# Three PSUM banks for the quads of a graph-attention loop, and one VectorE pass for a quad's keys

## The chip, the cores and the metric

One core of one Trainium2 chip runs the whole program. The metric is the device time of one execution in microseconds (us), the median over several executions.

## The reference

Four graph layers over 3,125 nodes of 64 features and 100,000 edges sorted by destination, each followed by a residual addition and a layer norm. The change lies in the last one, an attention whose logit of an edge is linear in the source row, the destination row and two edge attributes:

```python
z = h @ W_fc.T
a = z_src @ blk[0] + z_dst @ blk[K] + ex @ w_e      # + moment terms, the same for all edges
att = jnp.where(a > 0, a, SLOPE * a)
m = jax.ops.segment_max(att, dst, num_segments=N)
expv = jnp.exp(att - m[dst])
denom = jax.ops.segment_sum(expv, dst, num_segments=N)
w = expv / denom[dst]
msg = w[:, None] * (z_src + ez)
return jax.ops.segment_sum(msg, dst, num_segments=N)
```

## The kernel before

The last attention handles the edges in tiles of 128, 16 tiles (UT) to a unit, 49 units. Two kinds of unit run side by side.

**The first 28 units (ND)** need no gathered rows. A tile's weights are spread by one-hot matrices: `low_w` (128 edges by 128 low bits of the source, weighted) and `keys_w` (128 edges by 25*6 = 150 columns: high bits of the source and place of the destination in a window of 6). Their product over a quad of four tiles (QT) is summed in one PSUM bank of 25*20 = 500 columns; `weigh` on TensorE first clears the bank with a matmul by zeros (L2798), then makes the four products (L2806, each fp32 product is two instructions of the trace). VectorE adds the finished quad into `blocks` (`add_quad`, L2518). When the unit's four quads are added, `block_sum` (L2840) multiplies `blocks` with the node table `tab` and VectorE adds the result into `acc` (L2577).

**The other 21 units (NPU)** are gathered. GpSimd issues 16 indirect DMAs a unit (L2284), 334 in all, of rows of `att_tab[1]` into a ring of 7 slots (SLOTS), in a loop of its own; it waits for the landing of the first two of each four, and, from the eighth unit on, for the sum of the unit seven before. VectorE takes the logits out of the landed rows (`logits_p`: L2458, L2460, L2462) after waits on that unit's landings, ScalarE takes their exponents (L2679), VectorE scales one-hot windows (`hots_p`, L2503), TensorE sums (`gathered_sum`, L2829) and VectorE adds (L2570). Which gathered unit j is dealt with in which pass i of the main loop is the list `beside_of`: three in each four passes; unit 4 in pass 4, unit 11 in pass 13, unit 17 in pass 21, unit 20, the last, in pass 25.

The orders of the main loop are written by hand. VectorE in pass i: `turn_lo(i+2)` (L2349), `logits_d(i+1)` (L2467, L2470, L2472 and the three lines of the logits), `add_sums(i-1)`, `keys(i,2)`, `add_quad` 0, `keys(i,3)`, `add_quad` 1, 2 and 3, `keys(i+1,0)`, `keys(i+1,1)`, then `logits_p` and `hots_p` of the gathered unit. A call of `keys` first makes what `attributes` makes (L2485, L2487, after a wait for the products of the quad two before, since the rings of `low_w` and `keys_w` hold eight tiles) and then the four key tiles (L2511), each with a semaphore of its own. TensorE in pass i: `weigh(i)`, `sources(i+2)` (L2772), `block_sum(i)`, `gathered_sum`. Before quad m may clear its bank, TensorE waits until quad m-2 has been added: the banks 2 and 3 take turns. ScalarE makes `low_w` of three tiles of a quad (L2651, L2658), clears `blocks` and takes the exponents.

Bank 1 is used before the loop and in it only by a check of limits in passes 3 and 4. The banks 4 and 6 take the block sums (columns 0 to 87) by turns, 5 and 7 the gathered ones.

Of the kernel before, what the change touches and what calls it, by code (L numbers as in the profile page):

```python
# [8 lines left out]
ALU, ACT, AX = mybir.AluOpType, mybir.ActivationFunctionType, mybir.AxisListType  # L9

P = 128
N, D, E = 3125, 64, 100000
H, DH = 4, 16
NT = -(-N // P)
# [20 lines left out]
UT = 16  # L35
TW = 6
QT, QW = 4, 20
UW = 88
KH = NT * TW
# [4 lines left out]
LOW_RING = 8  # L44
# [22 lines left out]
def build(nc, x, src, dst, edge_attr_2, edge_attr_64, Wq, bq, Wk, bk, We, be, Wv, bv,  # L67
          attn_w, W_fc, W_attn, W_edge, W_e2n, W_m1, W_m2, out):
    ctx = ExitStack()
    with ctx:  # L70
        def sb(name, shape, dt=fp32):
            return ctx.enter_context(nc.sbuf_tensor(name, shape, dt))
# [7 lines left out]
        def short_sem(name):  # L80


            return nc.alloc_semaphore(name=name)

        def bc(ap, axis, n):

            ap = ap.unsqueeze(axis)
            shape = list(ap.shape)
            shape[axis] = n
            return ap.to_broadcast(shape)  # L90
# [20 lines left out]
        ident = sb("ident", [P, P])  # L111
# [65 lines left out]
        bank = [ctx.enter_context(nc.psum_tensor(f"bank{i}", [P, 512], fp32)) for i in range(8)]  # L177
# [771 lines left out]
        worst, worst_t = short_sem("worst_ready"), short_sem("worst_turned")  # L949
# [871 lines left out]
        def from_big(*shape):  # L1821

            size = int(np.prod(shape))
            view = big[:, at_big[0]:at_big[0] + size]
            at_big[0] += size
            assert at_big[0] <= big.shape[1]
            names = "abcd"[:len(shape)]
            return view if len(shape) == 1 else view.rearrange(f"p ({' '.join(names)}) -> p {' '.join(names)}", **dict(zip(names, shape)))

        TD = ND * UT  # L1830
        lo_t, hi_t, key_t = (from_big(TD) for _ in range(3))
# [26 lines left out]
        keys_w = shared[:, at_sh:at_sh + LOW_RING * KH].rearrange("p (r n) -> p r n", r=LOW_RING)  # L1858
# [13 lines left out]
        iota_k = shared[:, at_sh:at_sh + KH]  # L1872
# [12 lines left out]
        drift, drift2, root_of, extra_m, lim, lims, worst = (stage[:, a:b] for a, b in ((56, 57), (57, 58), (58, 59), (59, 60), (256, 264), (264, 280), (280, 288)))  # L1885
# [300 lines left out]
        def l2_pool(pool):  # L2186
# [19 lines left out]
        lo_ok3, u_ok3, u_used, arg_d, prob_d, arg_p, prob_p, attr_ok, hot_p, key_ok3, low_ok, main_ok, quad_added, cleared3, sum_d, rows_moved, sum_p, sum_p_added, ea_put = (  # L2206
            short_sem(f"e_{n}") for n in ("lo", "u", "u_used", "arg_d", "prob_d", "arg_p", "prob_p", "attributes", "hot_p", "key", "low", "main",
                                          "quad_added", "cleared", "sum_d", "rows_moved", "sum_p", "sum_p_added", "ea_put"))
# [25 lines left out]
            return slice((ND + i) * UT, (ND + i) * UT + tiles_of(i))  # L2234

        mean_cols = bank[7][:, D:D + 2]
        XP = [range(j, min(j + 4, -(-NT // 2))) for j in range(0, -(-NT // 2), 4)]

        ZG = [range(0, 14, 2), range(1, 14, 2), range(15, NT, 2), range(14, NT, 2)]
# [4 lines left out]
        def copy_x(engine, k):  # L2244


            js = XP[k]
            full = [j for j in js if 2 * j + 1 < NT]
# [24 lines left out]
        with nc.Block() as block:  # L2273
# [42 lines left out]
            def _(dve):  # L2316
# [40 lines left out]
                for g, ks in enumerate(WG):  # L2357
                    dve.wait_ge(win_ok, g + 1)
                    n, of = len(ks), slice(0, min(P, TL - ks[0] * P))
# [116 lines left out]
                def attributes(i, q):  # L2476

                    n, s = i * UT + q * QT, i % 2
                    at = n % LOW_RING
                    if q == 0:  # L2480
                        dve.wait_ge(prob_d, i + 1)
                    if n >= LOW_RING:
                        dve.wait_ge(main_ok, n + QT - LOW_RING)
                    last = at + QT - 1
                    nc.vector.tensor_scalar(low_w[:, last, 0:FREE], iota[:, 0:FREE], lo_t[:, n + QT - 1:n + QT], cols_d[:, 1, s, (q + 1) * QT - 1:(q + 1) * QT],  # L2485
                                            ALU.is_equal, ALU.mult).then_inc(attr_ok, 1)
                    nc.vector.tensor_tensor(low_w[:, at:at + QT, FREE:P], ea_t[:, n:n + QT, :], bc(cols_d[:, 1, s, q * QT:(q + 1) * QT], 2, 2),  # L2487
                                            ALU.mult).then_inc(attr_ok, 1)
# [16 lines left out]
                def keys(i, q):  # L2505

                    attributes(i, q)
                    for n in range(i * UT + q * QT, i * UT + (q + 1) * QT):
                        if n >= LOW_RING:
                            dve.wait_ge(main_ok, n - LOW_RING + 1)  # L2510
                        nc.vector.tensor_scalar(keys_w[:, n % LOW_RING, :], iota_k, key_t[:, n:n + 1], None, ALU.is_equal).then_inc(key_ok3, 1)  # L2511

                def add_quad(i, q, at):

                    n = i * (UT // QT) + q
                    dve.wait_ge(main_ok, (n + 1) * QT)
                    into = blocks[:, i % 2, :, bass.ds(at, QW)]
                    nc.vector.tensor_tensor(into, into, bank[2 + n % 2][:, 0:NT * QW].rearrange("p (h w) -> p h w", w=QW), ALU.add).then_inc(quad_added, 1)  # L2518
                    dve.drain()

                def registers(ap, most):
# [25 lines left out]
                def choose(i):  # L2547


                    if i == CHECK_AT:  # L2550
                        nc.vector.tensor_reduce(lims[0:5, 8:9], bank[1][0:5, 96:96 + P], AX.X, ALU.max)
                        nc.vector.tensor_scalar(lims[0:5, 9:10], ident[0:5, 4:5], -1.0, 1.0, ALU.mult, ALU.add)
                        nc.vector.tensor_copy(lims[0:5, 10:11], ident[0:5, 4:5])
                        dve.drain().then_inc(lim_top, 1)
                    if i == CHECK_AT + 1:
                        nc.vector.tensor_copy(worst[0:1, 0:2], bank[1][0:1, 96:98])
                        dve.drain()
                        nc.vector.tensor_scalar(worst[0:1, 2:3], worst[0:1, 0:1], SPREAD, None, ALU.is_gt)
                        dve.drain()
                        nc.vector.tensor_tensor(worst[0:1, 3:4], worst[0:1, 2:3], worst[0:1, 1:2], ALU.max)  # L2560
                        dve.drain()
                        nc.vector.tensor_copy(flag_i[:, 2:3], worst[0:1, 3:4])
# [140 lines left out]
            def _(pe):  # L2703
                for k, js in enumerate(XP):
                    for i, j in enumerate(js):
                        n = min(2, NT - 2 * j) * D
                        last = nc.tensor.transpose(bank[k][0:n, i * P:(i + 1) * P], xrow[:, 2 * j:2 * j + n // D, :].rearrange("p t f -> p (t f)"), ident[:, :])
                    last.then_inc(x_up, 1)
                for t in range(NT):
# [3 lines left out]
                    i = ZG[k].index(t)  # L2713
# [44 lines left out]
                def registers(ap, most):  # L2758

                    return nc.values_load_multi_w_load_instructions(ap, engines=[mybir.EngineType.PE], min_val=0, max_val=most,  # L2760
                                                                    skip_runtime_bounds_check_because="tables_dve holds them in this range")[1]
# [28 lines left out]
                def weigh(i):  # L2790

                    for q in range(UT // QT):
                        m = i * (UT // QT) + q
                        at = registers(quad_at[:, m * QT:(m + 1) * QT], QW - TW)
                        if m >= 2:
                            pe.wait_ge(quad_added, m - 1)
                        into = bank[2 + m % 2]
                        nc.tensor.matmul(into[:, 0:NT * QW], zeros_b[:, :], zero_cols(NT * QW), start=True, stop=False, skip_group_check=True)  # L2798
                        for j in range(QT):
                            n = m * QT + j  # L2800
                            if j == 0:
                                pe.wait_ge(attr_ok, 2 * (m + 1))
                            pe.wait_ge(key_ok3, n + 1)
                            if j < QT - 1:
                                pe.wait_ge(low_ok, m * (QT - 1) + j + 1)
                            nc.tensor.matmul(into[:, 0:NT * QW].rearrange("p (h w) -> p h w", w=QW)[:, :, bass.ds(at[j], TW)], low_w[:, n % LOW_RING, :],  # L2806
                                             keys_w[:, n % LOW_RING, :].rearrange("p (h w) -> p h w", w=TW), start=False, stop=j == QT - 1,
                                             skip_group_check=True).then_inc(main_ok, 1)

                def check_limits(i):  # L2810

                    if i == CHECK_AT:
                        pe.wait_ge(lim_ok, 1)
                        nc.tensor.transpose(bank[1][0:5, 96:96 + P], lim[:, 0:5], ident[:, :])
                    if i == CHECK_AT + 1:
                        pe.wait_ge(lim_top, 1)
                        nc.tensor.matmul(bank[1][0:1, 96:98], lims[0:5, 8:9], lims[0:5, 9:11], start=True, stop=True)

                def gathered_sum(j):

# [180 lines left out]
```

## Time and profile before

| | |
|---|---|
| median of 3 executions | 1918.82 us (1913.54 to 1918.93) |
| the profiled execution | 1916.29 us, span of its instructions 1914.5 us |
| VectorE busy | 1417.2 us, 74% |
| TensorE busy | 1365.9 us, 71% |
| GpSimd busy | 1241.5 us, 65% |
| main loop of the last attention | from 1458 to 1880 us of the span |

The busy shares are means over four layers with different limits. The loop of the last attention takes some 420 us of the span; what the change does is read there. Times in the rows are in us from the start of the span, of one profiled execution.

### The profile page before, as it was taken

To read this page: it belongs to the slowest core of one execution; us is meant where nothing else is said; L and a number is where in the kernel's file an instruction comes from. 1 tells how busy PE (TensorE), PEld (TensorE's weight loads), DVE (VectorE), ACT (ScalarE), POOL (GpSimd) and SP (SyncE) were. 2 spreads that over 40 slices of the span, in tenths; PEclk is the share of its full clock that TensorE was granted. 3 is DMA by queue.
4 is the path that set the end of the run, shared out by engine and by line. 5 is a ranking of instruction groups with operands and counts; after the bars stand their busy time and mean duration, and the time that the engine had idled before them with its cause. 6 is when DMAs were issued, how large, how long until landed. Compare 5 with 4: busy or idle time off the path is not lost. (4 is left out here: it accounts for less than half of the span.)

```text
span 1914.5 us, 44162 instructions
## 1 busy us (share of the span) xinstructions
PE 1365.9 (71%) x12903; PEld 1155.2 (60%) x12903; DVE 1417.2 (74%) x3785; ACT 1007.7 (53%) x2221; POOL 1241.5 (65%) x1328
## 2 busy tenths in 40 slices
PE   4476676676676767677776478648676788898884
PEld 3355555555555555555555378638576778888784
DVE  5777777777777777777777788788855777777774
ACT  2454444454454454454454295039724677777771
POOL 1677777777777777777777186025537777777740
PEclk8678878878888888888888688869966999999996
DMA  6333333333333333333332221000232222223210
GB/s 102 99 77 82 83 76 83 82 76 83 81 77 82 82 77 82 82 77 82 83 77 74 65 58 60 4 1 2 86 82 51 61 61 60 62 61 71 62 21 18
DMA packets 125228, 128.65 MB, mean 67 GB/s; under 512 B 80959, under 2 KB 88435, under 8 KB 124840
## 3 DMA queue, kind: packets, MB, share of 16 engines
q0 software_dynamic: 35776, 62.74, 15.9%
q1 hardware_dynamic: 63778, 57.41, 9.9%
q10 hardware_dynamic: 25542, 6.81, 1.6%
q8 instruction: 75, 1.23, 0.3%
q14 instruction: 57, 0.47, 0.1%
HBM read 116.64 MB, written 10.20 MB: 66 GB/s over the span
## 5 line engine op out<-in xcount | busy, mean ns | idle before, releaser
L636 POOL DMA_INDIRECT shared<-kv_tab,idx x784 | 767.7, 979 | 289.7 <-issue 237.7
L839 PE MATMUL bank<-key_hot,lo_hot 128*128 128x350 f16 x784 | 185.0, 341 | 299.2 <-DVE count L700 245.9
L2284 POOL DMA_INDIRECT count<-att_tab,count x240 | 237.4, 989 | 111.4 <-issue 70.7
L839 PEld LDWEIGHTS bank<-key_hot,lo_hot 128*128 128x128 f16 x784 | 56.0, 98 | 386.4 <-issue 371.2
L700 DVE TENSOR_TENSOR count<-count,bank 128x350 f32 x392 | 205.2, 523 | 82.4 <-issue 43.2
L772 ACT ACTIVATE lo_dist<-iota_neg,tile_lo 128x128 f16<-128x128 f32 x784 | 238.5, 389 | 0.0
L685 DVE TENSOR_SCALAR key_hot<-iota_key,tile_key 128x350 f16<-128x350 f16 x784 | 196.1, 320 | 0.0
L706 DVE TENSOR_TENSOR prod<-bank,shared 128x512 f32<-128x512 f32 x98 | 67.7, 691 | 149.1 <-DMA shared<-kv_tab,idx 141.0
L2806 PE MATMUL bank<-shared 128*128 128x150 f32 x896 | 159.4, 327 | 1.8 <-DVE shared L2511 1.8
L2658 ACT ACTIVATE shared<-shared 128x126 f32<-128x126 bf16 x336 | 143.3, 483 | 31.2 <-PE bank L2806 25.1
L814 PE MATMUL bank<-webd,eaT 128*128 128x128 f32 x784 | 159.1, 368 | 0.6 <-ACT eaT L766 0.6
L782 ACT ACTIVATE expo<-score 128x32 f32<-128x32 f32 x98 | 22.5, 229 | 254.7 <-DVE score L718 254.7
L854 PE MATMUL bank<-hots,msg 128*65 128x64 f32 x1568 | 154.7, 274 | 0.0
L854 PEld LDWEIGHTS bank<-hots,msg 128*65 128x65 f32 x1568 | 152.2, 189 | 0.4 <-DVE msg L727 0.4
L2806 PEld LDWEIGHTS bank<-shared 128*128 128x128 f32 x896 | 142.8, 216 | 15.0 <-issue 4.0
L766 ACT ACTIVATE eaT<-bank 128x512 f32<-128x512 f32 x98 | 58.6, 598 | 177.0 <-issue 177.0
L814 PEld LDWEIGHTS bank<-webd,eaT 128*128 128x128 f32 x784 | 145.6, 278 | 1.0 <-ACT eaT L766 1.0
L778 ACT ACTIVATE lo_hot<-lo_dist,small 128x1024 f16<-128x1024 f16 x98 | 112.5, 1148 | 25.5 <-issue 25.5
L822 PE MATMUL bank<-qwin,hotT 128*128 128x128 f32 x784 | 114.4, 289 | 0.0
L2840 PE MATMUL bank<-count,tab 128*68 128x88 f32 x1400 | 111.7, 240 | 1.8 <-DVE count L2518 1.8
L822 PEld LDWEIGHTS bank<-qwin,hotT 128*128 128x128 f32 x784 | 95.7, 192 | 25.3 <-issue 25.3
L2284 POOL DMA_INDIRECT g_edge<-att_tab,count x94 | 90.9, 967 | 29.3 <-issue 27.1
(528 smaller groups left out, 2974.7 us busy)
## 6 DMA issues: line engine op xcount, KB each, us to landing
shared<-in_edge_attr SPq DMA_DIRECT2D x97, 256.0 KB, 3.1
shared<-lo_tab SPq DMA_DIRECT2D x28, 512.0 KB
shared<-kv_tab,idx POOLq DMA_INDIRECT x784
count<-att_tab,count POOLq DMA_INDIRECT x240, 2.5
qwin<-q_tab ACTq DMA_DIRECT2D x196, 16.0 KB
kv_tab<-count SPq DMA_DIRECT2D x1, 1600.0 KB, 10.4
idx<-in_src SPq DMA_DIRECT2D x97, 4.0 KB, 1.6
g_edge<-att_tab,count POOLq DMA_INDIRECT x94
```

What stands on the lines that cost most here:

```text
L636: nc.gpsimd.indirect_dma_start(kv[:, s, c, :], None, kv_tab, bass.IndirectOffsetOnAxis(ap=idx[:, s, c:c + 1], axis=0)).then_inc(kv_in[s], 16)
L685: last = nc.vector.tensor_scalar(key_hot[:, c, :], iota_key[:, :], keys[:, c:c + 1], None, ALU.is_equal)
L700: nc.vector.tensor_tensor(at, at, bank[6 + q % 2][:, 0:KC].rearrange("p (h w) -> p h w", w=WC), ALU.add).then_inc(bank_free, 1)
L772: nc.scalar.activation(lo_dist[:, c, :], iota_neg[:, :], ACT.Abs, bias=los[:, c:c + 1])
L778: nc.scalar.activation(lo_hot[:, :, :], lo_dist[:, :, :], ACT.Relu, bias=edge_col, scale=-EDGE).then_inc(lo_ok, 1)
L814: nc.tensor.matmul(bank[3][:, q * P:(q + 1) * P], eaT[:, q * P:(q + 1) * P], webd[:, :], start=q == 0, stop=False, skip_group_check=True)
L822: last = nc.tensor.matmul(bank[4][:, c * D:(c + 2) * D], hotT[:, c // 2, :], qwin[:, s, :, :].rearrange("p a f -> p (a f)"), start=True, s ...
L839: last = nc.tensor.matmul(bank[6 + q % 2][:, 0:KC], lo_hot[:, c, :], key_hot[:, c, :], start=i == 0, stop=i == GT - 1)
L854: last = nc.tensor.matmul(bank[5][0:D + 1, 0:W], msg[:, c, :], hots[:, s % 2, c, :], start=c == 0, stop=c == C - 1)
L2284: nc.gpsimd.indirect_dma_start(ring[s][:, j, 0:D + 2], None, att_tab[1], bass.IndirectOffsetOnAxis(ap=src_i[:, t:t + 1], axis=0)).then_inc ...
L2658: nc.scalar.activation(low_w[:, n % LOW_RING, 0:FREE], low_dist[:, n % LOW_RING, 0:FREE], ACT.Relu, bias=p, scale=minus_p).then_inc(low_ok, 1)
L2806: nc.tensor.matmul(into[:, 0:NT * QW].rearrange("p (h w) -> p h w", w=QW)[:, :, bass.ds(at[j], TW)], low_w[:, n % LOW_RING, :], keys_w[:, ...
```

## The change

Three things are edited.

1. `quad_banks = (2, 3, 1)`: the quads take three banks by turns. TensorE waits for the addition of quad m-3 before it clears, where it waited for that of quad m-2.
2. The four `tensor_scalar` instructions of a quad's keys (128x150 each, one input, its compare value a column) become one `tensor_tensor` of 128x600 with two broadcast inputs, and one semaphore step. TensorE waits once for a quad's keys, ahead of the first product. The wait on `main_ok` inside the loop goes; the one in `attributes`, for the same ring, stays.
3. The check of limits moves from bank 1 to columns 96 and up of bank 4 or 6.

```diff
+        quad_banks = (2, 3, 1)
...
                     attributes(i, q)
-                    for n in range(i * UT + q * QT, i * UT + (q + 1) * QT):
-                        if n >= LOW_RING:
-                            dve.wait_ge(main_ok, n - LOW_RING + 1)
-                        nc.vector.tensor_scalar(keys_w[:, n % LOW_RING, :], iota_k, key_t[:, n:n + 1], None, ALU.is_equal).then_inc(key_ok3, 1)
+                    n = i * UT + q * QT
+                    at = n % LOW_RING
+                    nc.vector.tensor_tensor(keys_w[:, at:at + QT, :], bc(iota_k, 1, QT), bc(key_t[:, n:n + QT], 2, KH), ALU.is_equal).then_inc(key_ok3, 1)
...
-                    nc.vector.tensor_tensor(into, into, bank[2 + n % 2][:, 0:NT * QW].rearrange("p (h w) -> p h w", w=QW), ALU.add).then_inc(quad_added, 1)
+                    nc.vector.tensor_tensor(into, into, bank[quad_banks[n % 3]][:, 0:NT * QW].rearrange("p (h w) -> p h w", w=QW), ALU.add).then_inc(quad_added, 1)
...
-                        nc.vector.tensor_reduce(lims[0:5, 8:9], bank[1][0:5, 96:96 + P], AX.X, ALU.max)
+                        nc.vector.tensor_reduce(lims[0:5, 8:9], bank[4 + 2 * (i % 2)][0:5, 96:96 + P], AX.X, ALU.max)
...
-                        nc.vector.tensor_copy(worst[0:1, 0:2], bank[1][0:1, 96:98])
+                        nc.vector.tensor_copy(worst[0:1, 0:2], bank[4 + 2 * (i % 2)][0:1, 96:98])
...
-                        if m >= 2:
-                            pe.wait_ge(quad_added, m - 1)
-                        into = bank[2 + m % 2]
+                        if m >= 3:
+                            pe.wait_ge(quad_added, m - 2)
+                        into = bank[quad_banks[m % 3]]
...
                             if j == 0:
+                                pe.wait_ge(key_ok3, m + 1)
                                 pe.wait_ge(attr_ok, 2 * (m + 1))
-                            pe.wait_ge(key_ok3, n + 1)
...
-                        nc.tensor.transpose(bank[1][0:5, 96:96 + P], lim[:, 0:5], ident[:, :])
+                        nc.tensor.transpose(bank[4 + 2 * (i % 2)][0:5, 96:96 + P], lim[:, 0:5], ident[:, :])
...
-                        nc.tensor.matmul(bank[1][0:1, 96:98], lims[0:5, 8:9], lims[0:5, 9:11], start=True, stop=True)
+                        nc.tensor.matmul(bank[4 + 2 * (i % 2)][0:1, 96:98], lims[0:5, 8:9], lims[0:5, 9:11], start=True, stop=True)
```

## Rows read from the trace of the kernel before

**Rows 1.** The page's part 1: busy us (share of the span) xinstructions, by engine.
```profile
PE 1365.9 (71%) x12903; PEld 1155.2 (60%) x12903; DVE 1417.2 (74%) x3785; ACT 1007.7 (53%) x2221; POOL 1241.5 (65%) x1328
```

**Rows 2.** Windows in the loop: stretch, its length, busy us by engine, clock, DMA.
```profile
1600.00:1700.00 100.00, 89.67 (x1092) 82.97 (x1088) 78.45 (x275) 75.39 (x192) 74.48 (x78) 0.93 0.29 65
1700.00:1800.00 100.00, 90.25 (x1117) 83.22 (x1116) 77.35 (x268) 74.35 (x191) 75.00 (x77) 0.94 0.28 64
```

**Rows 3.** Waits of the loop, 1460 to 1880: waiter <- releaser: total, times, longest.
```profile
PE bank L2798 <- DVE count L2518: 44.1, 47, 7.0
DVE count L2518 <- PE bank L2806: 28.4, 30, 2.0
POOL count L2284 <- DMA count<-att_tab,count: 6.1, 7, 2.0
```

**Rows 4.** Timeline of VectorE in a pass: start, duration, instruction, [idle before <- releaser].
```profile
1660.36 0.35 DVE L2485 TENSOR_SCALAR shared<-iota,count,shared 128x126 f32<-128x126 f32 x1 [0.16 <-issue]
...
1671.20 0.92 DVE L2511 TENSOR_SCALAR shared<-shared,count 128x150 f32<-128x150 f32 x4
1672.04 0.67 DVE L2518 TENSOR_TENSOR count<-count,bank 128x500 f32 x1
1672.90 0.67 DVE L2518 TENSOR_TENSOR count<-count,bank 128x500 f32 x1 [0.20 <-issue]
1674.38 0.68 DVE L2518 TENSOR_TENSOR count<-count,bank 128x500 f32 x1 [0.81 <-PE bank L2806]
```

**Rows 5.** Timeline of TensorE in that pass.
```profile
1670.83 0.38 PE L2798 MATMUL bank<-zeros_b 128*128 128x500 f16 x1 [1.49 <-ACT shared L2658]
...
1672.98 1.26 PE L2806 MATMUL bank<-shared 128*128 128x150 f32 x8
1674.07 1.36 PE L2772 MATMUL bank<-shared,ad_row 128*128 128x25 bf16 x48
1675.28 3.99 PE L2840 MATMUL bank<-count,tab 128*68 128x88 f32 x50
```

**Rows 6.** VectorE timeline: two tensor_tensor instructions, fp32, inputs in SBUF.
```profile
1454.16 0.97 DVE L2451 TENSOR_TENSOR count<-count,edge_scratch 128x784 f32<-128x784 f32 x1
...
1664.83 0.57 DVE L2467 TENSOR_TENSOR shared<-count,iota 128x400 f32<-128x400 f32 x1
```

**Rows 7.** GpSimd timeline: last gathers of units 4, 11, 17 and 20, and two longer ones.
```profile
1521.68 0.94 POOL L2284 DMA_INDIRECT count<-att_tab,count  x1 [0.30 <-issue]
...
1617.80 1.00 POOL L2284 DMA_INDIRECT count<-att_tab,count  x1 [0.30 <-issue]
...
1663.79 1.24 POOL L2284 DMA_INDIRECT count<-att_tab,count  x1 [0.30 <-issue]
...
1666.58 0.94 POOL L2284 DMA_INDIRECT count<-att_tab,count  x1 [0.30 <-issue]
...
1791.17 0.94 POOL L2284 DMA_INDIRECT count<-att_tab,count  x1 [0.30 <-issue]
...
1849.37 0.94 POOL L2284 DMA_INDIRECT g_edge<-att_tab,count  x1 [0.30 <-issue]
```

**Rows 8.** VectorE timeline: first logits instruction of gathered units 4, 11, 17 and 20.
```profile
1542.58 0.17 DVE L2458 TENSOR_TENSOR shared<-count 128x16 f32<-128x16 f32 x1
...
1677.66 0.16 DVE L2458 TENSOR_TENSOR shared<-count 128x16 f32<-128x16 f32 x1
...
1794.98 0.18 DVE L2458 TENSOR_TENSOR shared<-count 128x16 f32<-128x16 f32 x1 [1.27 <-DMA count<-att_tab,count]
...
1852.79 0.18 DVE L2458 TENSOR_TENSOR shared<-g_edge,count 128x14 f32<-128x14 f32 x1
```

**Rows 9.** VectorE timeline: the last pass, two of its waits.
```profile
1869.75 0.34 DVE L2485 TENSOR_SCALAR shared<-iota,count,shared 128x126 f32<-128x126 f32 x1 [0.89 <-PE bank L2806]
...
1875.20 0.68 DVE L2518 TENSOR_TENSOR count<-count,bank 128x500 f32 x1 [0.80 <-PE bank L2806]
```

**Rows 10.** TensorE timeline: a quad's products after a long wait, in pass 3.
```profile
1518.47 2.21 PE L2806 MATMUL bank<-shared 128*128 128x150 f32 x8
```

## The prediction

> **What bounds the kernel now.** I read the page first, then windows, waits and timelines of the last attention, since only that loop (1458 to 1880) is touched. The page's shares [rows 1] name no bound. In two stretches of the loop TensorE is busy 90% and VectorE 78%, at a granted clock of 0.93 and 0.94 of full speed, nearly always the higher level [rows 2]; GpSimd is busy 75%, and that turns out to matter most.
>
> The waits point at the two banks: TensorE's clearing matmul waited 44.1 us for `add_quad`, and `add_quad` waited 28.4 us for the products [rows 3]. One pass shows how these join. VectorE begins a chain at 1660.36, and it runs nearly without a gap until the second addition, 1672.04 to 1672.71. Only then may TensorE clear the bank of the fourth quad, whose products run 1672.98 to 1674.24. The third addition is long done, and VectorE has been idle for 0.81 us when it starts the fourth at 1674.38, which ends at 1675.06 [rows 4, 5]. Behind it stand `block_sum` (1675.28) and the next pass. Between passes VectorE's order closes the ring: it is VectorE's work plus one trip to TensorE, some 14.86 us, where a pass has a gathered unit beside it. (The 1.49 us before the third quad's clearing is ascribed to ScalarE [rows 5], but the first addition, which the two-bank rule names, ended just before 1670.83.)
>
> There is a second ring, which neither edit touches. GpSimd issues the gathers one after the other, 0.94 to 0.95 us each and 0.30 us of issue between them. Its waits for landings make 6.1 us in 7 [rows 3], and the waits list none for a ring slot, so nothing that VectorE or TensorE do earlier makes it earlier. How far ahead is it? The last gather of unit 4 ends at 1522.62 and its logits begin at 1542.58: 20.0 us ahead. Unit 11: 1667.52 and 1677.66, 10.1 us. Unit 17: 1792.11 and 1794.98, and here VectorE waited 1.27 us for the landing. Unit 20, the last: 1850.31 and 1852.79, 2.5 us [rows 7, 8]. A landing takes up to some 2.9 us after the gather (unit 17, which did wait), so the lead is 17 us at unit 4 and nothing at 17 and 20. The loop already catches up with the gathers at its end.
>
> **The change part by part.**
>
> *Three banks.* The fourth quad need no longer wait for the second addition: its bank was freed by the addition of the first. Its products can start when its keys are there and the third quad's products are done. In the pass above the keys end at 1672.12 [rows 4], the products take 1.26 us [rows 5] and would end by 1673.5; VectorE meanwhile does the second and third additions and, after 0.20 us of its own issue, is ready for the fourth at 1673.77. The 0.81 us of idle time shrinks to these 0.20: 0.61 us a pass. What is late next is VectorE itself.
>
> *One pass for the keys.* The four old instructions take from 1671.20 to the start of the addition at 1672.04, 0.84 us, and show 0.92 us from first start to last end, since neighbours overlap by 0.08 [rows 4]. The trace has no 128x600 instruction of this form, but it has the same form at 400 columns, compare and two broadcast inputs included: 0.57 us; and a plain one at 784: 0.97 us [rows 6]. The line between them has 1.04 ns a column and gives 0.78 us at 600. Against 0.92 that is 0.14 us a quad. The bounds: all of the 784-column row (0.97, a loss of 0.05 a quad) and 0.57 + 0.10 (half the slope for the added columns, a gain of 0.25). I take 0.14, since the near row is the same operation. The wait for the gathers covers most of this term: only four quads come after it, so 0.97 us would move the end by 4 x 0.19 = 0.8 us; with that cover gone it would be 112 quads, 21 us. TensorE now waits for all four keys before the first product, where it could take them one by one; in the old order that freedom was unused, since the clearing came after all keys and an addition. Behind that wait stand the quad's four products; here it costs at most the order I have counted already.
>
> Together: 0.61 + 4 x 0.14 = 1.17 us a pass, and 28 x 1.17 = 33 us if the loop could have it all. TensorE has room for it: in that pass it was idle for 1.49 us before the third quad [rows 5].
>
> *The moved check* is one transpose, one small matmul and their readers in another bank, in the same places of the orders: nothing.
>
> *Where the gain meets the gathers.* Pass i runs up to 1.17 x (i+1) us earlier. By pass 9 or 10 this is 11 to 13 us, while the lead falls from 17 us (unit 4, pass 4) to 7 (unit 11, pass 13). From there on `logits_p` waits for its rows, a wait on VectorE with `hots_p` and the whole next pass queued behind it, and TensorE's `gathered_sum` behind that. Each later gain is given back at the next gathered unit. The logits of unit 20 cannot begin before the last gather's landing, and that stood at 1852.79 at most, at 1850.31 at least [rows 7, 8]. I take 0.2 us of this 2.5, since unit 17's landing took 2.9.
>
> *What is left* is what comes after unit 20: quads 2 and 3 of pass 26 and the fourth addition's idle time, 2 x 0.14 + 0.61, and the same in pass 27, where the same 0.80 us of idle time stands before the fourth addition [rows 9]. The keys of its quads 0 and 1 give nothing, because VectorE waits 0.89 us for TensorE after them [rows 9]. So 0.89 + 0.89 = 1.78, with the 0.2 above 1.98 us.
>
> *GpSimd's own pace* can shift the whole by a little. Some 24 gathers were stretched by 0.04 to 0.09 us while the old key instructions ran (one: 1.00 instead of 0.94) [rows 7]. If the new form doesn't, at most 1.2 us comes back; I take 0.6. The waits for landings (6.1 us, of which 0.30 each is issue) may fall otherwise by 2 or 3 us either way, since every transfer of the stage shifts. One at 1663.79, stretched to 1.24 us, is of another kind: it lies over `turn_lo`, a copy-like pass over 2,048 bf16 columns, and that stays.
>
> The sum: 1.98 + 0.6 = 2.6 us, so 1916.29 - 2.6 = 1913.7 for the profiled execution. The median of the runs is 2.5 us above that execution, which would give 1916.2; with single runs from 1913.54 to 1918.93 I take 1915.
>
> **The rivals.**
>
> *The full gain arrives.* If the gathers kept ahead all the same, 28 x 1.17 = 33 us: 1883. Against it stands that GpSimd works at 1.25 us a gather through the loop, and would have to issue its 334 gathers in some 30 us less.
>
> *GpSimd speeds up by itself.* Its landings fall better and the stretches go: 6 to 10 us, 1908 to 1912. It would need most of its landing waits to vanish.
>
> *Slower: the new form holds GpSimd back.* A gather reads its indices in SBUF, and the new keys instruction reads two SBUF inputs. If it blocks a gather as `turn_lo` does (0.30 us over the usual 0.94 [rows 7]), some 96 quads lie within the remaining gathers, and if each hits one, they end 29 us later: 1942. It decides from 0.03 us a quad on, where it eats my 2.6 us. Against it: the row of the same form at 400 columns (1664.83 to 1665.40 [rows 6]) lies over the gathers of its time, of which only the one before it, over `turn_lo`, was long.
> The Trainium skill, "SBUF — State Buffer", section "Who interferes with whom", states both sides: a VectorE instruction with two SBUF inputs contends with a GpSimd instruction that reads SBUF, whereas `tensor_scalar` can take a mode that locks the shared ports outright and `tensor_tensor` has none. By the first, this rival would hold; by the second, GpSimd would lose some stretches. The trace agrees with the second for bf16 `turn_lo` and shows next to nothing for the fp32 keys.
>
> *TensorE's clock.* TensorE will now stand idle ahead of the last gathered sums, for `hots_p`. After a wait of some 7 us the products of a quad took 2.21 us instead of 1.26 [rows 5, 10], the lower of the two levels (1.2 against 2.4 GHz). If that hits the fourth quads of passes 26 and 27, about 1 us each goes: no change at all, 1916 to 1918.
>
> **Chances.** The forecast (bound by the gathers, within 5.7 us of before, the clock's case with it): 0.75. GpSimd faster by itself: 0.11. The full gain or a large part: 0.06. GpSimd held back or another loss over 0.3%: 0.08. A measurement of this kernel tells about 0.3%, 5.7 us. So faster 0.17, same 0.75, slower 0.08. The range takes in GpSimd's faster case and 2 to 3 us of bad landings: 1908 to 1921; what it leaves out is the 0.06, most of the 0.08 and some edge.
>
> **What would show it.** VectorE's wait in front of the logits (L2458) on the gathers, 1.27 us before, should total some 20 to 30 us from the unit of pass 9 or 10 on. The idle time before `add_quad` should fall below half, the waits of the clearing matmul for `add_quad` should nearly vanish. The keys instruction should take 0.78 us. The last gather should end within 3 us of 1850.3. The prediction is wrong if the gathers end much earlier or later, or if `logits_p` doesn't wait.

## The result, and the profile after

The changed kernel takes 1931.81 us (median of 8, 1925.22 to 1935.70), the kernel before 1918.88 us (median of 8, 1913.54 to 1924.84). The ratio is 1.0061, with a 95% interval of 1.0041 to 1.0082: some 12 us slower. The forecast was 1915 us and no change, with a range of 1908 to 1921 us.

The profiled execution of the changed kernel took 1934.55 us, its span is 1932.8 us, 18.3 us more than before. Three stretches add up to that:

| stretch of the span | before | after | difference |
|---|---|---|---|
| start to the first gather | 1416.1 | 1420.8 | +4.7 |
| first gather's start to the last one's end | 434.3 | 448.4 | +14.2 |
| last gather's end to the end | 64.2 | 63.6 | -0.6 |

The first line is code that wasn't edited. Over the other profiled executions with all their gathers that start lies between 1414.5 and 1424.4, with no order in it; it is this execution's share of the spread between runs. The second line is the change.

VectorE's and TensorE's own part went as intended. The timeline of VectorE in a pass after the change, then TensorE's of the same pass:

```profile
1705.59 0.78 DVE L2511 TENSOR_TENSOR shared<-shared,count 128x600 f32<-128x600 f32 x1
1706.29 0.67 DVE L2518 TENSOR_TENSOR count<-count,bank 128x500 f32 x1
1707.15 0.68 DVE L2518 TENSOR_TENSOR count<-count,bank 128x500 f32 x1 [0.20 <-PE bank L2806]
1708.03 0.68 DVE L2518 TENSOR_TENSOR count<-count,bank 128x500 f32 x1 [0.20 <-PE bank L2806]
```

```profile
1703.73 0.37 PE L2798 MATMUL bank<-zeros_b 128*128 128x500 f16 x1
1704.71 1.28 PE L2806 MATMUL bank<-shared 128*128 128x150 f32 x8 [0.60 <-DVE shared L2511]
1705.83 0.37 PE L2798 MATMUL bank<-zeros_b 128*128 128x500 f16 x1
1706.50 1.29 PE L2806 MATMUL bank<-shared 128*128 128x150 f32 x8 [0.30 <-DVE shared L2511]
```

The keys take 0.78 us. The third and fourth clearing matmuls no longer wait (over the whole loop their waits for additions, 44.1 us before [rows 3], are gone), and TensorE now waits for the keys. The idle time before the fourth addition is 0.20 us where it was 0.81 [rows 4, 5].

What VectorE waits for in the loop, after (answering to [rows 3]):

```profile
DVE shared L2459 <- DMA count<-att_tab,count: 32.1, 7, 6.5
DVE shared L2486 <- PE bank L2806: 13.7, 16, 1.3
DVE acc L2577 <- issue: 12.9, 26, 0.9
DVE count L2518 <- PE bank L2806: 11.5, 50, 1.1
DVE shared L2459 <- DMA g_edge<-att_tab,count: 11.5, 4, 4.6
```

L2459 is the first instruction of `logits_p`. It waited 43.6 us for gathered rows, in 11 waits, where it had waited 1.3 us in one. So the time won was handed to the gathers, as forecast, and from gathered unit 5 (pass 5) on, earlier than the pass 9 or 10 that I gave; in the kernel with the banks only, below, the first long wait is in pass 9. VectorE's and TensorE's busy shares in the two stretches of [rows 2] fell accordingly:

```profile
1600.00:1700.00 100.00, 82.69 (x952) 77.44 (x953) 64.96 (x166) 68.91 (x174) 76.92 (x76) 0.86 0.26 59
1700.00:1800.00 100.00, 85.48 (x1012) 78.68 (x1011) 70.90 (x184) 73.35 (x189) 75.67 (x76) 0.91 0.27 64
```

The logits of units 11, 17 and 20 (answering to [rows 8]) stand behind waits of 4.6 to 6.5 us, and the last gather starts at 1868.27 where it started at 1849.37 [rows 7], 18.9 us later, where the forecast allowed 3:

```profile
1683.82 0.18 DVE L2459 TENSOR_TENSOR shared<-count 128x16 f32<-128x16 f32 x1 [6.49 <-DMA count<-att_tab,count]
...
1810.46 0.18 DVE L2459 TENSOR_TENSOR shared<-count 128x16 f32<-128x16 f32 x1 [5.41 <-DMA count<-att_tab,count]
...
1871.36 0.18 DVE L2459 TENSOR_TENSOR shared<-g_edge,count 128x14 f32<-128x14 f32 x1 [4.56 <-DMA g_edge<-att_tab,count]
```

```profile
1868.27 0.94 POOL L2285 DMA_INDIRECT g_edge<-att_tab,count  x1 [0.30 <-issue]
```

Why are the gathers slower? Their groups, of the changed kernel and of the kernel before, in the stretch 1400 to 1900 (count, busy us, mean ns, idle before):

```profile
L2285 POOL DMA_INDIRECT count<-att_tab,count x240 | 246.4, 1027 | 110.0 <-issue 69.8 <-DMA att_tab<-tab 34.0 <-DMA count<-att_tab,count 5.7
L2285 POOL DMA_INDIRECT g_edge<-att_tab,count x94 | 95.3, 1014 | 30.7 <-issue 27.7 <-DMA g_edge<-att_tab,count 2.7 <-DMA count<-att_tab,count 0.3
```

```profile
L2284 POOL DMA_INDIRECT count<-att_tab,count x240 | 237.4, 989 | 111.4 <-issue 70.7 <-DMA att_tab<-tab 34.7 <-DMA count<-att_tab,count 6.1
L2284 POOL DMA_INDIRECT g_edge<-att_tab,count x94 | 90.9, 967 | 29.3 <-issue 27.1 <-DMA g_edge<-att_tab,count 2.2
```

The idle times are the same; the instructions are longer, by 246.4 + 95.3 - 237.4 - 90.9 = 13.4 us. Set beside VectorE's timeline, it is plain which ones. GpSimd, then VectorE, after:

```profile
1716.75 0.94 POOL L2285 DMA_INDIRECT g_edge<-att_tab,count  x1 [0.30 <-issue]
1718.00 1.03 POOL L2285 DMA_INDIRECT g_edge<-att_tab,count  x1 [0.30 <-issue]
1719.33 1.49 POOL L2285 DMA_INDIRECT g_edge<-att_tab,count  x1 [0.30 <-issue]
1721.13 0.94 POOL L2285 DMA_INDIRECT g_edge<-att_tab,count  x1 [0.31 <-issue]
```

```profile
1717.44 0.78 DVE L2511 TENSOR_TENSOR shared<-shared,count 128x600 f32<-128x600 f32 x1
...
1719.23 0.78 DVE L2511 TENSOR_TENSOR shared<-shared,count 128x600 f32<-128x600 f32 x1
```

The gather of 1719.33 starts 0.10 us into a keys instruction that has 0.68 us to go, and takes 1.49 us, 0.55 more than its neighbours. The one of 1718.00 meets the last 0.22 us and takes 0.09 more. Counted over the whole trace, 50 of the 334 gathers start under a keys instruction; 36 of them have more than 0.13 us of it to go, and all but one of these are longer than 0.945 us by that rest less 0.11 to 0.13 us. Together it is 13.5 us. A gather under which a keys instruction starts later is not longer, but for one of 68, which is recorded as starting 0.03 us ahead of the instruction and is 0.71 us longer. So a gather that starts under the instruction waits for its end.

The old keys held gathers by the same rule, only for less. The gather of 1617.80 in the kernel before, one of the two longer ones of [rows 7], took 1.00 us. It started 0.10 us into this instruction, with 0.18 us to go:

```profile
1617.70 0.28 DVE L2511 TENSOR_SCALAR shared<-shared,count 128x150 f32<-128x150 f32 x1
```

Of the 53 gathers there that started with more than 0.13 us of an old keys instruction to go, 27 are longer by that rest less 0.12 to 0.14 us, together 1.4 us. Another 23 started within 0.06 us of the instruction's own start and are longer by 0.02 us at most. The last 3 are 0.21 to 0.31 us longer, and two of these also meet `turn_lo`.

A gather is held only to the end of the instruction under which it starts, although the next one of the four starts 0.08 us before that end. So four instructions of 0.29 us hold one by 0.13 us at most, and one of 0.78 us holds it by up to 0.63.

`turn_lo`, 0.75 us long and with one SBUF input, holds a gather that starts under it by the same rule (9 of 14 in the kernel before; the other 5 started within 0.04 us of its start). It also holds gathers already under way: the one of 1663.79 [rows 7] started 0.37 us before it and ends 0.12 us after it. Of the 15 gathers that `turn_lo` met so, 11 were longer, and each of these ended 0.12 us after it.

### The profile page after: what moved, and what is told of

The parts are those of the page before. It is cut to its first block and busy times, and to the rows that moved or that the text cites. A ratio compares the mean times of both kernels' runs of the same rounds, so it can differ in the third digit from the quotient of the medians.

```text
span 1932.8 us, 43602 instructions
## 1 busy us (share of the span) xinstructions
PE 1382.7 (72%) x12903; PEld 1183.8 (61%) x12903; DVE 1400.0 (72%) x3449; ACT 1008.6 (52%) x2221; POOL 1253.3 (65%) x1328
## 5 line engine op out<-in xcount | busy, mean ns | idle before, releaser
L839 PE MATMUL bank<-key_hot,lo_hot 128*128 128x350 f16 x784 | 180.3, 334 | 292.0 <-DVE count L700 244.9
L2285 POOL DMA_INDIRECT count<-att_tab,count x240 | 246.4, 1027 | 110.0 <-issue 69.8
L2806 PEld LDWEIGHTS bank<-shared 128*128 128x128 f32 x896 | 146.7, 218 | 45.2 <-issue 38.3
L854 PE MATMUL bank<-hots,msg 128*65 128x64 f32 x1568 | 167.0, 288 | 0.0
L854 PEld LDWEIGHTS bank<-hots,msg 128*65 128x65 f32 x1568 | 165.4, 203 | 0.4 <-DVE msg L727 0.4
L2285 POOL DMA_INDIRECT g_edge<-att_tab,count x94 | 95.3, 1014 | 30.7 <-issue 27.7
```

Source lines behind the costliest of these rows:

```text
L839: last = nc.tensor.matmul(bank[6 + q % 2][:, 0:KC], lo_hot[:, c, :], key_hot[:, c, :], start=i == 0, stop=i == GT - 1)
L854: last = nc.tensor.matmul(bank[5][0:D + 1, 0:W], msg[:, c, :], hots[:, s % 2, c, :], start=c == 0, stop=c == C - 1)
L2285: nc.gpsimd.indirect_dma_start(ring[s][:, j, 0:D + 2], None, att_tab[1], bass.IndirectOffsetOnAxis(ap=src_i[:, t:t + 1], axis=0)).then_inc ...
```

## The experiments

Theory G: the gathers bind the loop, and the new keys instruction stretches the gathers that start under it, because it reads two inputs from SBUF. Rival B: the three banks or the new order of waits slow the loop itself. Rival P: the loss lies ahead of the loop.

| kernel | median us | ratio to before (95%) | gathers: us, stretch | logits waited |
|---|---|---|---|---|
| before | 1918.88 | 1 | 434.3, 12.9 | 1.3 |
| changed | 1931.81 | 1.0061 (1.0041 to 1.0082) | 448.4, 26.6 | 43.6 |
| banks only | 1916.30 | 0.9986 (0.9965 to 1.0007) | 434.1, 12.5 | 21.3 |
| keys only | 1930.59 | 1.0070 (1.0049 to 1.0092) | 452.8, 31.4 | 32.1 |
| keys only, one input in PSUM | 1914.26 | 0.9982 (0.9963 to 1.0001) | 431.0, 12.6 | 13.5 |
| changed, half the gathers | 1869.46 | 0.9756 (0.9728 to 0.9783) | 380.9, 24.6 (168 of them) | 0 |
| before, half the gathers | 1914.58 | 0.9977 (0.9956 to 0.9998) | 367.1, 8.4 (168) | 0 |

Each ratio is to runs of the kernel before on the same chip (medians 1918.7 to 1920.3 us); it is not the quotient of two medians, and lies up to some 0.002 from it. Stretch is the sum over all gathers of the time above 0.945 us. Some 12 us of it stand in each kernel with all its gathers, most of it from other lines: in the kernel before 5.6 us belong to gathers held by `turn_lo`.

**Banks only.** The changed kernel with the old keys, and TensorE waiting for them one by one as before:

```diff
-                    nc.vector.tensor_tensor(keys_w[:, at:at + QT, :], bc(iota_k, 1, QT), bc(key_t[:, n:n + QT], 2, KH), ALU.is_equal).then_inc(key_ok3, 1)
+                    for n in range(i * UT + q * QT, i * UT + (q + 1) * QT):
+                        if n >= LOW_RING:
+                            dve.wait_ge(main_ok, n - LOW_RING + 1)
+                        nc.vector.tensor_scalar(keys_w[:, n % LOW_RING, :], iota_k, key_t[:, n:n + 1], None, ALU.is_equal).then_inc(key_ok3, 1)
...
-                                pe.wait_ge(key_ok3, m + 1)
...
+                            pe.wait_ge(key_ok3, n + 1)
```

> Three banks and the moved check, the keys in four tensor_scalar instructions as before. Theory G (the loop is bound by GpSimd's gathers, and the new keys instruction stretches those gathers that start under it): the gathers take 434 us from the first start to the last end, as before, and the time is that of before or 1 to 3 us less (1916 to 1919). Rival B (the three banks or the new order of waits make the loop slower): the time stays near that of the changed kernel, 10 us or more above before. Rival P (the loss comes from ahead of the loop, where nothing was edited): first gather late by 4 us or more here too.

As theory G has it. The banks cost nothing; what they win, VectorE spends waiting for rows, in the logits:

```profile
DVE shared L2459 <- DMA count<-att_tab,count: 19.2, 5, 5.0
```

**Keys only.** The kernel before, with the one-pass keys and its single wait on TensorE; banks 2 and 3.

> Two banks as before, the keys in one tensor_tensor. Theory G: some 0.3 to 0.4 of a gather in each ten is stretched, the gathers take 10 to 15 us longer than in before (445 to 449), time 8 to 14 us above before. Rival B: the time of before, or a few us less by 4 x 0.14 us a pass.

The whole loss is back with the keys alone. 55 gathers start under the instruction and are 18.4 us longer in sum; the gathers take 452.8 us, somewhat more than the 445 to 449 expected. Banks only has shown that the three banks do no harm. This kernel has the single wait for four keys as well, so it leaves open whether that wait does; the next one settles it. Rival P falls here: the first gather starts at 1416.9, within 1 us of before, and the loss is there.

**Keys only, one input in PSUM.** As above, with the check of limits moved as in the change, and:

```diff
+        iota_ps = bank[1][:, 0:KH]
...
+                nc.vector.tensor_copy(iota_ps, iota_k)
+                dve.drain()
...
-                    nc.vector.tensor_tensor(keys_w[:, at:at + QT, :], bc(iota_k, 1, QT), bc(key_t[:, n:n + QT], 2, KH), ALU.is_equal).then_inc(key_ok3, 1)
+                    nc.vector.tensor_tensor(keys_w[:, at:at + QT, :], bc(iota_ps, 1, QT), bc(key_t[:, n:n + QT], 2, KH), ALU.is_equal).then_inc(key_ok3, 1)
```

> Two banks (2 and 3); the keys in one tensor_tensor as in the changed kernel, but its first input, the 150 column numbers, is read from PSUM bank 1, so that it has one SBUF input like the addition of a quad, under which no gather was stretched. Theory G: the stretches under the keys vanish (0 us), the gathers take 432 to 436 us, time that of before or up to 2 us less. If instead the length of the instruction or its one pass does the harm, whatever its inputs: 8 to 14 us above before, as with the keys alone.

The instruction is as long as before, and harmless. Its group, and a gather that starts 0.10 us into one, with 0.68 us to go, like that of 1719.33 above:

```profile
L2513 DVE TENSOR_TENSOR shared<-bank,count x112: 768/776/784, 1460.0 to 1869.1; 128x600 f32<-128x600 f32 x112
```

```profile
1632.26 0.78 DVE L2513 TENSOR_TENSOR shared<-bank,count 128x600 f32<-128x600 f32 x1
```

```profile
1632.36 0.94 POOL L2285 DMA_INDIRECT count<-att_tab,count  x1 [0.30 <-issue]
```

64 gathers start with more than 0.13 us of such an instruction to go and are 1.0 us longer in sum, against 13.5 us for 36 in the changed kernel. All of the 1.0 us is in four gathers under which `turn_lo` starts next, and each ends 0.12 us after `turn_lo`. Length, number and order are those of the keys-only kernel. Only the place of one input differs, beside the check in passes 3 and 4 and one copy ahead of the loop. The single wait on TensorE is there too and does no harm, so rival B has fallen, and with it my remark in the forecast that this wait might matter. The gathers take 431.0 us, 1 less than expected. The time is 3.5 us below before by the ratio, where I had up to 2, and its interval still takes in no change.

The Trainium skill ("SBUF — State Buffer", section "Who interferes with whom") states this rule: a VectorE instruction with two SBUF inputs contends with a GpSimd instruction that reads SBUF. The traces agree with it, 13.5 us against 1.0.

So theory G holds but for its reason. That both inputs lie in SBUF is needed for the new form to hold gathers. It isn't what sets the new form apart from the old, which reads one input from SBUF and holds them too; that is its length. The new compare in four pieces of 150 columns would show how much is length alone, and was not run.

**Half the gathers.** The changed kernel, with the tiles 2 and 3 of each four of a gathered unit left out:

```diff
+                for s in range(SLOTS):
+                    nc.gpsimd.memset(ring[s][:, :, 0:D + 2], 1.0)
+                pool.drain()
...
+                        if j % 4 > 1:
+                            continue
...
-                        if j % 4 == 3:
+                        if j % 4 == 1:
...
-                    dve.wait_ge(rows3_last[j % SLOTS], last_rows(j, n))
```

> The changed kernel with half the gathers left out (tiles 2 and 3 of each four of the 21 gathered units; their places in the ring are filled with ones once), so its output differs. Theory G: GpSimd is far ahead, the logits never wait, and the loop shows its own speed: a pass of 13.7 us with a gathered unit and 11.4 without, 30 us or more below before (1880 to 1890), although the keys instruction is the same. If the loop itself had become slower or the gathers were not its bound: the time stays within 10 us of the changed kernel, above before.

No wait for rows is left, and the stretched gathers (24.6 us over 168) cost nothing. The time is 10 us and more below the expected 1880 to 1890.

**Half the gathers, before.** The same edit in the kernel before.

> The kernel before (two banks, four key instructions) with the same half of the gathers left out and the ring filled with ones once, so its output differs. Theory G: the loop's own ring, 14.9 us a pass with a gathered unit, is what binds, and the gathers cost it only the 1.3 us of one wait: 1905 to 1917, and 31 to 38 us above the changed kernel with half the gathers (28 passes by 0.61 + 4 x 0.14 us, and fewer stretches at the lower clock). If half the gathers alone explained the gain of that run, the two would lie within 10 us.

The time is in the expected range, the distance to the kernel above is not: 1914.58 to 1869.46 is 45 us. What the change does to the loop when no gather binds it is less than that. From the start of the first block sum to that of the last it is 403.5 us before and 368.2 after, 35.3 us over 27 passes; the forecast had 27 x 1.17 = 31.6. The two profiled executions are 46.1 us apart. Of the rest 6.7 us lie ahead of the first block sum, 5.2 of them ahead of the first gather where nothing was edited, and 4.0 behind the last, with no cause shown. Passes with a gathered unit take 13.6 to 14.3 us from pass 7 on, but for the last of them; one of 13.67 us, seen from the starts of two block sums in the changed kernel with half the gathers:

```profile
1796.79 3.99 PE L2844 MATMUL bank<-count,tab 128*68 128x88 f32 x50
1810.46 3.99 PE L2844 MATMUL bank<-count,tab 128*68 128x88 f32 x50
```

The forecast's steps give 14.86 - 1.17 = 13.69.

**Moving the bound.** If the gathers bind, work should go from GpSimd to the loop. ND says how many units are dense; each step takes 16 gathers away and adds a pass. The edit is one constant, in three forms of the kernel:

| ND | before | banks only | changed |
|---|---|---|---|
| 28 | 1 | 0.9986 | 1.0061 |
| 29 | | 0.9901 (0.9875 to 0.9926), 1901.67 us | 0.9953 (0.9931 to 0.9975), 1908.41 us |
| 30 | 1.0081 (1.0049 to 1.0113), 1933.05 us | 0.9932 (0.9908 to 0.9956), 1906.58 us | 0.9923 (0.9898 to 0.9947), 1902.39 us |
| 31 | | 1.0006 (0.9980 to 1.0032), 1918.61 us | |

> Three banks, four key instructions, and ND = 30 for 28: two gathered units (32 gathers, 40.5 us of GpSimd) become dense ones. Theory G: the last gather ends near 1808 us of the span and no longer binds; the loop's own end moves from 1843 (estimate) by two passes of 11.4 us less two gathered parts of 2.3 us to some 1861 less what the last gathers freed; time 1885 to 1898, 20 to 30 us below before. If the gathers were not the bound: 18 us slower than with ND = 28.

> The changed kernel, one tensor_tensor for the keys, with ND = 30 for 28. Theory G: the stretches of gathers stay (12 to 16 us in all) but cost little where the gathers have a lead, and the shorter keys of VectorE (0.14 us a quad) now count: within 8 us of the one with four key instructions and ND = 30, 15 to 30 us below before. A rival in which the one-pass keys harm the loop by another way (TensorE waiting for all four keys): slower than that one by 10 us or more.

> Three banks, four key instructions, ND = 31. Theory G: the loop itself is the bound beyond the balance, so a third moved unit costs one more dense pass, some 9 us, and gives nothing back: 5 to 10 us above ND = 30.

> Three banks, four key instructions, ND = 29 for 28. By theory G both bounds lie near each other: 318 gathers at the pace of the banks-only kernel (434.1 us for 334) end near 1829 us of the span, and the loop's own end, from the 1872.7 of ND = 30 less a pass of 12, is near 1861; the block sums of the last pass would start at 1855 to 1862, time 1893 to 1901, 18 to 25 us below before and not above ND = 30.

> The changed kernel with ND = 29. Theory G: the stretched gathers (448.4 us for 334) end near 1843 us and bind again, time 1903 to 1912: the one-pass keys lose to the four instructions with ND = 29 and win with ND = 30, since it is only where the gathers have a lead that VectorE's saving counts.

> The kernel before (two banks, four key instructions) with ND = 30 alone. Theory G: without the three banks the loop's own ring binds, 14.9 or 12.7 us a pass, so two more dense passes less two gathered parts cost 18 to 22 us: 1935 to 1942, above before. If moving units is the whole gain of the ND = 30 kernels: 1900 to 1910.

The signs are as theory G has them, but that the one-pass keys win at ND = 30 is not clear of noise; the sizes are not all right. With the two banks the moved units only cost. With three banks they win until the loop itself binds. The changed kernel keeps its stretched gathers (413.3 us for 302, against 400.1 in the one with four key instructions), loses at ND = 28, 29 by that, and has caught up at 30, where its logits waited 2.8 us in all. With four key instructions and three banks the time for ND = 30 lies 8.6 us above what I expected, ND = 31 costs 12.0 us more than that where I had 5 to 10, and ND = 29 is 0.7 us above its range; the times of the other two forms lie in or within 2 us of their ranges. I had taken the pass of 13.6 us from the kernel with half the gathers, which has the short keys. The starts of the block sums tell the two apart, four key instructions first:

```profile
1807.55 4.01 PE L2841 MATMUL bank<-count,tab 128*68 128x88 f32 x50 [0.32 <-DVE count L2519]
1821.79 4.01 PE L2841 MATMUL bank<-count,tab 128*68 128x88 f32 x50
```

```profile
1794.01 3.99 PE L2840 MATMUL bank<-count,tab 128*68 128x88 f32 x50
1807.65 3.99 PE L2840 MATMUL bank<-count,tab 128*68 128x88 f32 x50
```

14.24 us against 13.64, a difference of 0.60, and the shorter keys were to give 4 x 0.14 = 0.56. These are single passes, though: from the first block sum to the last it is 400.4 us against 390.5, 9.9 us over 29 passes or 0.34 each. Of the two fastest, ND = 29 with banks only and ND = 30 with the change, the intervals overlap; both beat the kernel before, by some 15 to 19 us.

## Why the prediction was wrong

- *The bound.* Right: the loop was on the point of being held by the gathers, and what the banks and the keys won turned into VectorE's wait for rows (43.6 us).
- *Three banks, 0.61 us a pass.* Right: the idle time went from 0.81 to 0.20. Alone they gave 0.9986, or 2.7 us, which is not clear of no change; it is the 2 us that were to be left after the last gather.
- *Keys, 0.78 us.* Right (0.776).
- *GpSimd's own pace, a gain of 0.6 us.* This is the step that failed. It rests on the forecast's statement that neither edit touches the ring of the gathers, and the new keys do. The new keys were to give GpSimd 0.6 us back; the gathers took 14.2 us more. I had it as the rival "the new form holds GpSimd back", with a chance of 0.08 and a price of 29 us. The price was for all of 96 quads at 0.30 us each; in fact one gather in seven starts under the instruction, and loses 0.27 us on average (13.5 us over 50). The trace of before, with its row of 1454.34 shown below, allowed a better price, as an estimate: an instruction of 0.78 us holds a gather that starts at a random place in it by the rest less 0.13, and a gather comes every 1.30 us (434.3 over 334). That gives 0.65 x 0.65 / (2 x 1.30) = 0.16 us a quad, 17 us over the 106 quads before the last gather; the changed kernel lost 13.5, the keys-only one 18.4. By this estimate the loss grows with the square of the length beyond 0.13 us.
- *The evidence against that rival was no evidence.* I took the 400-column row of [rows 6] and saw that the gather of its time was not stretched. That gather started 0.06 us before the instruction's end. All 12 gathers that started under this line in the trace of before had 0.06 us or so of it to go, less than the 0.13 us below which nothing shows. The other row of [rows 6], 784 columns with two SBUF inputs at 1454.16, did have a gather start under it, and the trace of before says what became of it:

```profile
1454.34 1.61 POOL L2284 DMA_INDIRECT count<-att_tab,count  x1 [0.30 <-issue]
```

  1.61 us instead of 0.94: the rest of 0.79 less 0.13. I priced VectorE's side from that row and never looked at GpSimd's at the same time. I also read the trace as showing next to nothing for the old fp32 keys. It shows the hold, cut short by the end of a short instruction; of some 27 gathers longer by 0.04 to 0.09 us (I had counted 24) 18 started under an old keys instruction.
- *What is left after unit 20.* The part behind the last gather is 1.4 us shorter with the banks only (62.8 us) and 0.6 in the changed kernel, where I had 1.98. The part up to the start of the last block sum is the one that the edits can reach: 25.6 us before, 24.4 with the banks only, 26.1 in the changed kernel, so there nothing of the 1.98 arrived. TensorE, idle for the rows, did the first two quads of pass 26 in 2.21 us instead of 1.29, at a granted clock of 0.54 from 1876 to 1882. This was the rival of TensorE's clock, which had named the fourth quads of passes 26 and 27; that the clock is what ate the gain fits, and no run shows it alone:

```profile
1876.25 2.21 PE L2806 MATMUL bank<-shared 128*128 128x150 f32 x8
1878.25 0.62 PE L2798 MATMUL bank<-zeros_b 128*128 128x500 f16 x1
1878.67 2.21 PE L2806 MATMUL bank<-shared 128*128 128x150 f32 x8
```

- *The profiled execution's start*, 4.7 us later, is not part of the ratio's 12 us and was not explained.

## What to carry to other kernels

When an edit speeds up a loop, look for the engine that runs a loop of its own beside it, and plot its lead over the waits that consume it: here it fell from 17 us to nothing, and said where the gain would end. Then ask what the edit does to that engine; here that was the cost that decided. One instruction of 0.78 us held the gathers for more than four did that took 0.92 us together, because a gather gets in between the four. To judge whether instruction X holds back engine Y, take only the pairs in which Y starts while X has long to go; a pair that merely overlaps proves nothing. With the bound known, moving work off it was worth more than both edits: 1.0061 became 0.9923 by one constant, and 0.9901 with the banks and ND = 29, without the new keys.

## What the runs showed of the hardware

- An indirect DMA instruction of GpSimd that starts under a VectorE `tensor_tensor` with two SBUF inputs is longer by the rest of that instruction less 0.13 us (rest 0.76, longer by 0.63; rest 0.68, by 0.55). With one of the inputs in PSUM it isn't (rest 0.68, longer by 0).
- Within some 0.06 us the recorded order of the two doesn't tell which is held. In the changed kernel a gather that started 0.01 us after the keys instruction was not longer, with 0.81 us to go, and one that started 0.03 us ahead of one was longer by 0.71 us. A gather that started earlier than that was not held by a keys instruction.
- The bf16 `turn_lo` (`tensor_scalar`, 0.75 us) also holds a gather that is under way: in the kernel before, 11 of 15 that started ahead of it end 0.12 us after it.
- The four fp32 `tensor_scalar` instructions of 128x150, with one SBUF input, hold a gather as well, each by its own rest less 0.13 us: 27 of 53 in the kernel before, 1.4 us together. Under the additions of the quads, with one input in PSUM, none of 35 gathers there and none of 45 in the changed kernel was longer.
